# Two split passes instead of three for the gram product of a mixture-of-experts part, with x plus its low part as VectorE's factor

## The reference

```python
h_norm = layer_norm(h, rn_g, rn_b)
g = softmax(einsum('bsd,ed->bse', h_norm, router_w))
top2_w, top2_idx = top_k(g, 2)            # of 4 experts
hid = einsum('bsd,edh->bseh', h, w1)      # 128 -> 4 x 256
hid = relu(layer_norm(hid, ln_g, ln_b))
expert_out = einsum('bseh,ehd->bsed', hid, w2)
out = sum(top2_out * top2_w)
return layer_norm(out, on_g, on_b)
```

## Time and profile before

| | |
|---|---|
| runs of the kernel | 991.92, 992.06, 993.33 us (median 992.06) |
| profiled execution: span from first to last instruction | 992.1 us |
| VectorE busy | 887.5 us |
| TensorE busy | 948.7 us |
| ScalarE busy | 828.9 us |
| GpSimd busy | 94.7 us |
| mean granted TensorE clock | 0.990 of full |

### The profile page before, as it was taken

The page is one execution under the profiler, slowest core; times in us unless marked ns, Lnnn a source line. Parts: engine busy times, 40 slices in busy tenths (PEclk is TensorE's granted clock), DMA queues, the critical chain, the costliest instruction groups (busy, mean ns, idle before and its releaser), DMA issues.

```text
span 992.1 us, 13389 instructions
## 1 busy us (share of the span) xinstructions
PE 948.7 (96%) x3582; PEld 604.7 (61%) x3582; DVE 887.5 (89%) x2332; ACT 828.9 (84%) x1361; POOL 94.7 (10%) x99
## 2 busy tenths in 40 slices
PE   8799999999999999999999999999999989999996
PEld 7356555555555555555555555655555557777785
DVE  7779999999999999999999999999998778888887
ACT  6789999999999999999989999999998864445535
POOL 1000000000000000000001000000001020333320
PEclk9899999999999999999999999999999999999998
DMA  9000000000000000020000000000000200000001
GB/s 344 4 0 1 1 1 0 1 1 1 0 1 1 1 1 1 1 85 1 1 1 5 2 1 1 1 1 1 1 1 1 85 1 1 12 12 12 12 12 33
DMA packets 8232, 15.86 MB, mean 16 GB/s; under 512 B 992, under 2 KB 5472, under 8 KB 8032
## 3 DMA queue, kind: packets, MB, share of 16 engines
q1 hardware_dynamic: 7728, 14.82, 4.2%
q10 hardware_dynamic: 432, 0.20, 0.1%
HBM read 12.92 MB, written 2.10 MB: 15 GB/s over the span
## 4 chain that ended last, share of the span: by engine, by line
PE 59%; ACT 20%; DVE 10%; issue 10%; DMA 1%; SPq 0%; ACTq 0%; DVEq 0%
PE Oa L965 12%; PE R L859 6%; PE Ob L965 6%; PE R L861 5%; PE R L860 5%; ACT L685 4%; PE SV L1006 4%; ACT rs L525 3%; PE Ob L920 3%; ACT L729 3%; ACT rz L504 2%; ACT hid L544 2%; DVE V L1693 2%; PE Ca L985 1%; ACT expq L487 1%
## 5 line engine op out<-in xcount | busy, mean ns | idle before, releaser
L544 ACT ACTIVATE hid<-R,par 128x512 f32<-128x512 f32 x224 | 148.5, 698 | 14.2 <-PE R L861 12.2
L965 PE MATMUL Oa<-hid,wraw 128*128 128x512 f32 x256 | 134.7, 608 | 2.7 <-ACT hid L544 1.1
L965 PE MATMUL Ob<-hid,wraw 128*128 128x512 f32 x256 | 130.9, 592 | 0.0
L859 PE MATMUL R<-x_h,wf_h 128*128 128x512 f32 x224 | 105.9, 473 | 0.5 <-ACT hid L544 0.5
L525 ACT ACTIVATE rs<-SV,eps_ln 128x512 f32<-128x512 f32 x128 | 88.3, 690 | 9.1 <-PE SV L1006 5.7
L859 PE MATMUL R<-xr_h,wqkv_h 128*128 128x512 f32 x156 | 87.9, 563 | 2.9 <-DVE Kt L1374 1.1
L1418 DVE SCALAR_TENSOR_TENSOR y<-x,par,y 128x512 f32<-128x512 f32 x120 | 87.5, 748 | 3.4 <-ACT y L553 3.1
L1429 DVE TENSOR_TENSOR y_l<-y,y_h 128x512 fp32r<-128x512 f32 x128 | 87.8, 686 | 1.2
L860 PE MATMUL R<-x_l,wf_h 128*128 128x512 f32 x224 | 88.0, 393 | 0.0
L861 PE MATMUL R<-x_h,wf_l 128*128 128x512 f32 x224 | 88.0, 393 | 0.0
L530 ACT ACTIVATE rs<-rs 128x512 f32<-128x512 f32 x128 | 80.7, 631 | 1.2
(11 more groups left out here) (298 smaller groups left out, 2387.9 us busy)
## 6 DMA issues: line engine op xcount, KB each, us to landing
wraw<-w_dram SPq DMA_DIRECT2D x7, 768.0 KB, 12.5
x<-x_dram SPq DMA_DIRECT2D x8, 256.0 KB, 6.9
Q<-x_dram SPq DMA_DIRECT2D x1, 2048.0 KB, 7.8
out_dram<-reluq SPq DMA_DIRECT2D x6, 256.0 KB, 2.3
wraw<-w_dram SPq DMA_DIRECT2D x2, 512.0 KB, 5.2
wraw<-w_dram SPq DMA_DIRECT2D x1, 576.0 KB, 7.4
wraw<-row_dram SPq DMA_DIRECT2D x1, 512.0 KB, 4.7
wraw<-bias_dram SPq DMA_DIRECT2D x1, 512.0 KB, 6.1
```

The costliest lines, as they stand in the source:

```text
L544: nc.scalar.activation(hid[:, m * CH:(m + 1) * CH], HIDDEN[m][:, :], GELU, bias=param(u // 4, BF1 + m % FB)).then_inc(hid_done, 1)
L859: nc.tensor.matmul(bank, w_h, a_h, start=True, stop=False)
L965: mm = nc.tensor.matmul(O[h][:, :], raw(u // 4, WF2 + j * P, P), hid[:, m * CH:(m + 1) * CH], start=(j == 0), stop=(j == FB - 1))
```

## The change

TensorE drops the pass low by high (x's low part by the gram matrix's high part). ScalarE makes x rounded to float32r (`high_xt`), VectorE makes 2x - high from it, which is x plus its low part (`twice_x`), in place in the buffer `expq`, and `squares` multiplies by that instead of by x. Since G is symmetric, (G high) · (x + low) has the cross term twice, once for each side.

```diff
@@ names
+        xt_h = expq[:, :].bitcast(F32R)
+        x_twice = expq
@@ ScalarE
+            def high_xt(it, k):
+                n = upto_chunk(it, k)
+                act.wait_ge(xt_done, n * TILES)
+                after(act, square_done, (n - 2) * TE)
+                nc.scalar.activation(xt_h[:, half(k % 2)], xt[:, half(k % 2)], ACT.Copy).then_inc(xt_h_done, 1)
@@ ScalarE, end_of_layers
                 high_x(0, 0)
                 gelu_hidden(last, 6)
+                high_xt(0, 0)
                 square(1, last - 1, 1)
...
                 high_x(0, 1)
+                high_xt(0, 1)
                 log_var(1, last - 1, 1)
@@ ScalarE, step, after the eight relus
+                if enters:
+                    high_xt(it, k + 1)
                 if routes:
                     roots_of_hidden(it, k)
                     exp_logits(it, k)
@@ TensorE, gram
                 nc.tensor.matmul(g[:, :], xe_h[:, par_tile(k, t)], gram_h, start=True, stop=False)
-                nc.tensor.matmul(g[:, :], xe_l[:, par_tile(k, t)], gram_h, start=False, stop=False)
                 nc.tensor.matmul(g[:, :], xe_h[:, par_tile(k, t)], gram_l, start=False,
                                  stop=True).then_inc(gram_mm, 1)
@@ VectorE
+            def twice_x(it, k):
+                n = upto_chunk(it, k)
+                c = half(k % 2)
+                dve.wait_ge(xt_h_done, n)
+                nc.vector.scalar_tensor_tensor(out=x_twice[:, c], in0=xt[:, c], scalar=2.0, in1=xt_h[:, c].bitcast(F32),
+                                               op0=ALU.mult, op1=ALU.subtract).then_inc(x_twice_done, 1)
             def squares(it, k, t):
                 n = upto_chunk(it, k)
+                dve.wait_ge(x_twice_done, n)
                 dve.wait_ge(gram_mm, (n - 1) * TILES + t + 1)
...
-                                                   in1=xt[:, par_tile(k, t)], op0=ALU.mult, op1=ALU.mult,
+                                                   in1=x_twice[:, par_tile(k, t)], op0=ALU.mult, op1=ALU.mult,
@@ VectorE, end_of_layers
                 low_square(1, last - 1, 1)
+                twice_x(0, 0)
                 weave(squares(0, 0, 0))
...
                 low_x(0, 1)
+                twice_x(0, 1)
@@ VectorE, step
                     split_std(it, k)
                 if enters:
+                    twice_x(it, k + 1)
                     low_x(it, k + 1)
```

More of the change, by code:

```diff
@@ L259, in build @@
         xe_l_done = sem("xe_l_done")
+        xt_h_done = sem("xt_h_done")
+        x_twice_done = sem("x_twice_done")
         router_mm = sem("router_mm")
```

## The result

The changed kernel takes 996.14 us (median of 4 runs, 994.98 to 996.51), the kernel before 991.99 (4 runs, 991.79 to 993.33): the ratio is 1.004, 95% interval 1.0028 to 1.0051. So it is slower, by 4.15 us or 0.4%, where 2.85 us was forecast; 996.14 lies inside the predicted range. The profiled execution took 996.29 us with a span of 994.4.

The account below looks back on a forecast made before the run. A middle step was taken as bound by VectorE's statistics, GpSimd's L2162 holding VectorE, then gapless VectorE work. -0.4 - 0.2 + 4.0 - 0.15 - 0.4 = +2.85 on 992.06 gave 994.9 us, range 991.8 to 997.0.

Parts of the forecast that it names:

- first stage: Chunks 1 and 2, beside the last layer: delays and the lock's stall cancel; sum -0.4 us, between -1.5 and +1.2.
- chunk 2, pass and one new instruction: Step of chunk 2: dropped TensorE pass -0.2 us, one new VectorE instruction +0.67 us; together +0.47.
- five more new instructions: VectorE's remaining new instructions, in its stretch without gaps ahead of low_x: 0.67 us each, +3.35 us.
- race at the lock: Middle steps: VectorE and GpSimd SBUF instructions shut each other out; order decides long or 0.4 us shorter steps; -0.4 us.
- ScalarE, all steps short: Middle steps: ScalarE's rounding costs nothing, 0; 0.1 us in a step in which L1621 is stalled.
- chunk 8: Last step with gram products: VectorE waits for TensorE, but L2162 limits L1610's earlier start; -0.15 us, at most -0.7.
- Rival 2: Middle steps: TensorE's longer waits make its clock fall, +3.5 us more, 998.4 us; chance 0.06.
- long form: Middle step in which GpSimd holds L1614, three of five before; all five long priced at +0.8 us.
- short step: Middle step in which L1614 slips in ahead and L1621 is held, 0.4 us shorter; two of five before.
- signs of being wrong: Middle step not longer, L1607's earlier start reaching L1625, ScalarE's exponential later than VectorE asks, or middle-step clock below full.
- Rival 1: TensorE's saving comes through: 985.3 us, chance 0.05; weak form, only the pass ahead of the router: 993.8 us, 0.12.
- Rival 3: Lock's stalls disappear, L1610 and L1614 both before L2162, first stage's stall gone too: 993.0 us; chance 0.13.

Follow-up runs that it names:

- e2: Kernel before with the low-by-high pass left out of all 32 gram products, squares still by x: 989.79 us against 991.16, ratio 0.9975 to 0.9992.
- e4: Kernel before with VectorE's eight new instructions alone (three passes, no ScalarE roundings): 995.72 us against 991.16, ratio 1.0033 to 1.0062.
- e6: Changed kernel with GpSimd instead of VectorE making 2x less high x in six steps: 991.99 us against 991.72 for the kernel before.
- e9: Changed kernel run again with nothing edited: 995.94 us against 991.92 for the kernel before, ratio 1.0024 to 1.0048.
- e5: Changed kernel with ScalarE's rounding of x moved behind the roots and exponential in six steps: 994.20 us against 991.72 for the kernel before.
- e10: Changed kernel with chunk 1 alone as in the kernel before: 994.41 us against 991.92 for the kernel before, ratio 1.0014 to 1.0034.
- e3: Kernel before with ScalarE's eight roundings alone (three passes, squares by x): 992.10 us against 991.16, ratio 0.9993 to 1.0013.
- e7: Kernel before (three passes) without GpSimd's two 128x512 instructions beside the gating, output not the reference's: 988.52 us against 991.72.
- e1: Kernel before run again with nothing edited: 991.14 us against 991.16.
- e11: Changed kernel with chunk 1 as before, GpSimd making 2x less high x in chunks 3 to 8 and waiting in chunk 2's step: 990.49 us against 991.92.

## Why the prediction was right, and where it was not

The direction and its reason held. VectorE's new work is paid in every middle step, and TensorE's saving shortens none of the short ones (e2, e4, e6). The terms by their measured sizes, from the two traces of the kernel before and the two of the changed one:

| term | forecast | measured |
|---|---|---|
| first stage | -0.4 (-1.5 to +1.2) | +1.4 (A: mean 17.40 less 15.96) |
| chunk 2, pass and one new instruction | +0.47 | +0.45 |
| five more new instructions | +3.35 | +3.0 (0.60 each) |
| race at the lock | -0.4 | -1.4 (0.39 for each of 3 and 4 long steps) |
| pause ahead of L1686, chunk 6 to 7 | none | -0.35 |
| ScalarE, all steps short | 0 | +0.4 (0.08 a step) |
| chunk 8 | -0.15 | -0.2 |
| sum | +2.85 | +3.3 |

The five middle steps take 108.9 and 109.3 us before and 110.8 and 110.6 after, +1.6, which is what the four rows for them come to. The medians are 4.15 and (e9) 4.0 apart, so up to 0.9 us between profiled and other executions isn't assigned.

- **The first stage is the step that failed.** It came out 1.8 us above its term and outside its own bounds. The prediction had `squares` of chunk 1 starting 1.15 us later, TensorE done 0.7 earlier and the stall at the lock moved on to L1610, all of which came (1.24, 0.87, and 1.03 us for L1633), and concluded that `low_x` of chunk 2 comes as before; it came 1.51 us later. What it didn't follow is `low_y`, which stands behind these `squares` in VectorE's queue and for which TensorE already waited 0.43 us. The wait grew to 2.56 us, the clock fell within it, 0.3 us (after) to 1.2 us (e9) before its end, and the products behind it ran at half clock. All four traces of kernels with the whole change in chunk 1 (after, e5, e6, e9) show waits of 2.56 to 2.60 us, half the clock behind them and a first stage of 16.8 to 17.9 us; the nine others show 15.3 to 16.3. e10 shows the cause to be what the change does to chunk 1. How much of it is the late start and how much the clock is worked out from rows and not shown by a run, but either alone costs nothing that can be seen: in e3 and e4 the product starts 0.5 and 0.7 us late at full clock (first stage 15.40 and 15.27), in e2 it is on time and half clock follows from 809.4 to 815.9 (15.52). Rival 2 had the right mechanism in the wrong place: the middle steps, where it was priced, kept the full clock at waits of 0.91 us. (Its 2.7 us at half clock don't come out of its row either: a mean of 0.66 over 5 us is 3.4 us at half clock.)
- **The race was mis-sized.** That L1610 would meet L2159 and be let in at that instruction's end was right. That the winner is then settled was not seen; I took a third of the gain where all of it came.
- **The new instruction costs 0.60, not 0.67.** The price was read from an instruction that also takes a number for each partition (`par`). That kind is 0.75 us long and costs 0.66 to 0.67 in the rows of the first stage too (L1432, 807.63 to 808.29 and 811.83 to 812.50), whatever follows it; the new one is 0.68 long. The lower bound, a TENSOR_TENSOR of this size, was the right row.
- **ScalarE's part at nothing** held in the long form. For a short step the prediction named 0.1 us but put none in its sum; 0.08 came (e5), and all steps turned short.
- **The sum is better than its parts, and that is luck.** The first stage missed by +1.8 us and ScalarE by +0.4; the race by -1.0, the price of the new instruction and the pause by -0.35 each.
- **Two of its own signs of being wrong showed**: one middle step (chunk 6 to 7) isn't longer, since the pause went, and ScalarE's exponential starts some 0.1 us later than VectorE asks for it (VectorE's L1644 ends at 899.20, L651 starts at 899.34).
- **Rival 1** is out: 7.3 us of TensorE's work went and e2 is only 1.6 us faster by its ratio, most of it through the race. **Rival 3** came by half: in every middle step L1610 and L1614 are both through before L2162. The stall in the first stage stayed, and L1621 is held in their place; e7 shows that the whole lock was worth 3.2 us.

What stays open: why the low clock lasts 3 us in one trace of the changed kernel and 10 in the other. Nor is it clear on what it hangs whether the clock falls ahead of the first gram product of chunk 2: of the five traces with the same three waits of 0.4, 1.0 and 0.7 us ahead of it, it falls in before, e7 and e10 and stays full in e1 and e11.
